# GELU of stages 0 to 2 built from the hyperbolic tangent, with other engines doing the operations around it and the MLP work in later slots

## The reference

```python
def gelu(x):                                     # stage 1; stage 2 uses jax.nn.gelu(x, approximate=True), the same
    return 0.5 * x * (1.0 + jnp.tanh(0.7978845608028654 * x * (1.0 + 0.044715 * x * x)))
...
ln_out = layernorm(x, ln3_s, ln3_b)              # stage 1
mlp_out = gelu(ln_out @ w1 + b1) @ w2 + b2       # 256 -> 1024 -> 256
return x + mlp_out
...
out = rmsnorm(attn_out, postnorm_w)              # stage 2
out = jax.nn.gelu(out @ mlp_w1 + mlp_b1) @ mlp_w2 + mlp_b2
return out + residual
```

## Time and profile before

| what | value |
|---|---|
| median of 3 runs | 2325.23 us (2323.97 to 2326.45) |
| the profiled execution | 2326.19 us |
| its span, first to last instruction | 2324.5 us |
| mean granted clock of PE | 0.961 |
| PE busy | 2114.0 us (91%) |
| DVE busy | 1292.8 us (56%) |
| ACT busy | 1257.4 us (54%) |
| POOL busy | 680.7 us (29%) |

### The profile page before, as it was taken

The page is one execution under the profiler, slowest core; times in us unless marked ns, Lnnn a source line. Parts: engine busy times, 40 slices in busy tenths (PEclk is TensorE's granted clock), DMA queues, the critical chain, the costliest instruction groups (busy, mean ns, idle before and its releaser), DMA issues.

```text
span 2324.5 us, 43553 instructions
## 1 busy us (share of the span) xinstructions
PE 2114.0 (91%) x14880; PEld 1810.9 (78%) x14880; DVE 1292.8 (56%) x4117; ACT 1257.4 (54%) x3924; POOL 680.7 (29%) x618
## 2 busy tenths in 40 slices
PE   4788999999999999897699999999799999999788
PEld 3667777777777777675599999999689999999677
DVE  3658575858576665433455555555545555555654
ACT  2466777786868776644444444444444444444432
POOL 2223333323333333322322222213322221222353
PEclk8899999999999999997799999999999999999989
DMA  6000000000000000000100000000000000000100
GB/s 237 1 4 11 1 10 1 11 1 9 2 2 10 1 4 1 3 1 1 49 24 23 23 18 23 14 23 23 16 24 18 23 14 23 23 23 14 37 14 23
DMA packets 23663, 45.23 MB, mean 19 GB/s; under 512 B 2400, under 2 KB 10080, under 8 KB 22624
## 3 DMA queue, kind: packets, MB, share of 16 engines
q1 hardware_dynamic: 21440, 32.62, 4.5%
q10 hardware_dynamic: 1440, 8.72, 0.9%
q0 software_dynamic: 640, 2.10, 0.3%
HBM read 41.33 MB, written 2.10 MB: 19 GB/s over the span
## 4 chain that ended last, share of the span: by engine, by line
PE 22%; issue 22%; POOL 5%; DVE 2%; ACT 1%; POOLq 0%; ACTq 0%; DVEq 0%
PE general L1573 15%; PE o_psum L1622 2%; PE scores L1610 2%; PE general L1729 2%; POOL probs L1219 1%; POOL w_qk L1195 1%; PE pT_psum L1670 1%; POOL hT L1210 1%; DVE oT L1555 1%; POOL X L1235 1%; POOL w_v L1195 1%; POOL w_o L1195 0%; POOL vrow L1199 0%; DVE oT L1424 0%; ACT oT L1334 0%
## 5 line engine op out<-in xcount | busy, mean ns | idle before, releaser
L430 POOL TENSOR_TENSOR probs<-probs,rsums 128x512 f32<-128x512 f32 (+1 forms) x288 | 283.9, 992 | 670.2 <-DVE rsums L631 669.1
L1219 POOL TENSOR_TENSOR probs<-probs,rsums 128x512 f32<-128x512 f32 x128 | 133.2, 1040 | 764.3 <-DVE rsums L1417 764.3
L470 ACT ACTIVATE probs<-negated,negmax 128x128 f32<-128x128 f32 (+1 forms) x768 | 326.2, 429 | 49.3 <-DVE negmax L622 48.4
L914 PE MATMUL pT_psum<-ident,probs 128*128 128x128 f32 x1088 | 181.8, 290 | 62.1 <-DVE probsT L637 34.4
L1326 ACT COPY probsT<-pT_psum 128x512 f32<-128x512 f32 x128 | 74.9, 585 | 288.8 <-PE pT_psum L1670 288.8
L914 PEld LDWEIGHTS pT_psum<-ident,probs 128*128 128x128 f32 x1088 | 134.0, 148 | 110.6 <-issue 75.2
L1573 PE MATMUL general<-hT,w_qk 128*128 128x512 f32 x768 | 207.0, 405 | 4.2 <-POOL hT L1210 4.2
L1573 PE MATMUL general<-w_o,oT 128*128 128x256 f32 x1536 | 194.6, 281 | 17.0 <-DVE oT L1424 17.0
L1573 PEld LDWEIGHTS general<-w_o,oT 128*128 128x128 f32 x1536 | 186.0, 188 | 25.3 <-DVE oT L1424 18.1
L1573 PE MATMUL general<-ctxT,w_qk 128*128 128x512 f32 x768 | 200.5, 397 | 0.0
L1318 ACT ACTIVATE probs<-scores,negmax 128x128 f32<-128x128 f32 x512 | 180.1, 369 | 29.8 <-DVE negmax L1409 29.7
(11 more groups left out here) (173 smaller groups left out, 4211.2 us busy)
## 6 DMA issues: line engine op xcount, KB each, us to landing
raw_qk<-w_qk_dram SPq DMA_DIRECT2D x34, 256.0 KB, 2.7
raw_v<-w_v_dram SPq DMA_DIRECT2D x17, 256.0 KB, 2.6
raw_vrows<-vrows_dram SPq DMA_DIRECT2D x17, 256.0 KB, 3.2
weights_a<-weights_a_dram ACTq DMA_DIRECT2D x2, 2048.0 KB, 17.7
raw_o<-w_o_dram SPq DMA_DIRECT2D x16, 256.0 KB, 2.6
weights_a<-weights_a_dram ACTq DMA_DIRECT2D x3, 1024.0 KB, 10.0
X<-x_dram SPq DMA_DIRECT2D x8, 256.0 KB, 7.4
ctx_in<-ctx_dram SPq DMA_DIRECT2D x8, 256.0 KB, 4.5
```

Source lines behind the costliest of these rows:

```text
L430: nc.gpsimd.tensor_tensor(pr, pr, rsums[:, n % 4, 0:segs].unsqueeze(2).broadcast_to([P, segs, width(kind) // segs]), ALU.mult).then_inc(s[ ...
L470: last = nc.scalar.activation(probs[:, n % PROBS, i * wide:(i + 1) * wide], src[:, i * wide:(i + 1) * wide], ACT.Exp, scale=1.0 if kind == ...
L914: last = nc.tensor.transpose(pT_psum[:, j * P:(j + 1) * P], probs[:, n % PROBS, j * P:(j + 1) * P], ident[:, :])
L1219: nc.gpsimd.tensor_tensor(pr, pr, rsums[:, t % 2, :].unsqueeze(2).broadcast_to([P, NB, P]), ALU.mult).then_inc(s["probs_ready"], 1)
```

## The change

- The GELU is computed as y (1 + tanh(c y (y y + s))) with y the pre-activation, and the factor 0.5 is applied in the residual sum. ACT writes y to `upT` with `Identity` (`pre_activations`). POOL computes y y, adds s, multiplies by y into the new tile `inner` (`gelu_argument`, in the slot of the up-projection, as the last thing of the slot). ACT applies `Tanh` with a scale to it one slot later (`tanh`), DVE computes (t + 1) y two slots later (`gelu_product`, before the slot's first work).
- The down-projection waits for the product of `up3` (`gelu_ready`).
- `WORK`: the MLP's ups of stage 1 go from slots 24 to 27 to 26 to 29, its downs from 29, 30 to 32, 33; the downs of stage 2 go from 58, 59 to 60, 61; `lat`, `lat_q`, `lat_k` go from 32, 33, 34 to 34, 35, 35; `cross_k` from 8 to 4 and `cross_v` from 13 to 5. The order within slots changes too.
- `ctx_in` and `xhat` have one buffer each; SP loads ctx 1 after all of x, and each later one waits for the group before.

```diff
-        ("mlp2_down0", 58),
-        ("ln3", 23), ("mlp2_down1", 59),
-        ("chan_q", -12), ("chan_k", -12), ("mlp1_up0", 24),
-        ("self_o", 7), ("chan_v", -11), ("mlp1_up1", 25),
-        ("mlp1_up2", 26), ("cross_k", 8),
-        ("ln2", 9), ("mlp1_up3", 27),
-        ("cross_q", 10),
-        ("mlp1_down0", 29),
-        ("mlp1_down1", 30),
-        ("cross_v", 13),
-        ("ln1", -4), ("lat", 32),
-        ("self_q", -3), ("lat_q", 33),
-        ("self_k", -2), ("lat_k", 34),
-        ("self_v", -1), ("lat_o", 53)]
+        ("cross_k", 4),
+        ("ln3", 23), ("cross_v", 5),
+        ("chan_q", -12), ("chan_k", -12), ("mlp2_down0", 60),
+        ("self_o", 7), ("mlp2_down1", 61), ("chan_v", -11),
+        ("mlp1_up0", 26),
+        ("ln2", 9), ("mlp1_up1", 27),
+        ("cross_q", 10), ("mlp1_up2", 28),
+        ("mlp1_up3", 29),
+        ("ln1", -4), ("mlp1_down0", 32),
+        ("self_q", -3), ("mlp1_down1", 33),
+        ("lat", 34), ("self_k", -2),
+        ("lat_q", 35), ("lat_k", 35), ("self_v", -1), ("lat_o", 53)]
+
+GELU_ARGUMENT, GELU_TANH, GELU_PRODUCT = 0, 1, 2
...
-        ctx_in = sb("ctx_in", [P, 2, NA, D])
-
-        xhat_of = {"x": sb("xhat_x", [P, NA, D]), "y": sb("xhat_y", [P, NA, D])}
+        ctx_in = sb("ctx_in", [P, NA, D])
+
+        xhat = sb("xhat", [P, NA, D])
...
+        inner = sb("inner", [P, 2, 2 * RA])
...
+                def gelu_argument(name, g):
+                    i, y, t = up_parts(name, g)
+                    wait_copied(pool, name, g)
+                    wait_count(pool, s["gelu_ready"], i - 1)
+                    nc.gpsimd.tensor_tensor(t, y, y, ALU.mult).then_inc(s["gelu_step"], 1)
+                    pool.wait_ge(s["gelu_step"], 2 * i + 1)
+                    nc.gpsimd.tensor_scalar(t, t, GELU_SHIFT, None, ALU.add).then_inc(s["gelu_step"], 1)
+                    pool.wait_ge(s["gelu_step"], 2 * i + 2)
+                    nc.gpsimd.tensor_tensor(t, t, y, ALU.mult).then_inc(s["argument_ready"], 1)
...
-                        ins = nc.scalar.activation(upT[:, f, :], src[:, j * RA:(j + 1) * RA], ACT.Gelu_apprx_tanh, bias=col(name + "_b", f))
+                        ins = nc.scalar.activation(upT[:, f, :], src[:, j * RA:(j + 1) * RA], ACT.Identity, bias=col(name + "_b", f))
                     ins.then_inc(freed, 1)
+
+                def tanh(name, g):
+                    i, _, t = up_parts(name, g)
+                    act.wait_ge(s["argument_ready"], i + 1)
+                    nc.scalar.activation(t, t, ACT.Tanh, scale=GELU_SCALE).then_inc(s["tanh_done"], 1)
...
+                def gelu_product(name, g):
+                    i, y, t = up_parts(name, g)
+                    dve.wait_ge(s["tanh_done"], i + 1)
+                    nc.vector.scalar_tensor_tensor(out=y, in0=t, scalar=1.0, in1=y, op0=ALU.add, op1=ALU.mult).then_inc(s["gelu_ready"], 1)
...
                         wait_free(pe, name + "_down", g)
-                        for i in (2, 3):
-                            wait_copied(pe, f"{name}_up{i}", g)
+                        pe.wait_ge(s["gelu_ready"], UPS.index((name + "_up3", g)) + 1)
```

More of the change, by code:

```diff
@@ L74 @@
 NEG = -1.0e30
+GELU_CUBIC = 0.044715
+GELU_SHIFT = 1.0 / GELU_CUBIC
+GELU_SCALE = 0.7978845608028654 * GELU_CUBIC
 RSQRT_MAGIC = 1597463007.0
@@ L127, in at_slot, with ups_at @@
             if (slot - after) % PERIOD == 0 and 0 <= (slot - after) // PERIOD < GA]
+def ups_at(slot):
+    return [(name, g) for name, g in at_slot(WORK, slot) if "_up" in name]
 def pair_at(slot):
@@ L145 @@
 ADD_ORDER = [item for slot in SLOTS for item in at_slot(ADDS, slot)]
+UPS = [(name, g) for name, g in WORK_ORDER if "_up" in name]
 MASKED_UNITS = [key for key in UNIT_INDEX if key[0] in ("self", "cross")]
@@ L250, in stages_0_to_2 @@
         ctxT_loaded = [sem(f"ctxT_loaded{i}") for i in range(B // NB)]
-        ctx_loaded = [sem(f"ctx_loaded{i}") for i in range(2)]
         mask_cross_loaded = [sem(f"mask_cross_loaded{i}") for i in range(2)]
@@ L447, in _ @@
                         normalise(kind, g, 2 * p + 1)
+                    for name, g in ups_at(slot - GELU_ARGUMENT):
+                        gelu_argument(name, g)
             @block.scalar
@@ L569, in _ @@
                         copy_out(name, g)
+                    for name, g in ups_at(slot - GELU_TANH):
+                        tanh(name, g)
             @block.vector
@@ L678, in norm @@
                     inverse_root()
-                    xhat = xhat_of[STREAM[name]]
+                    before = NORM_ORDER.index((name, g)) - 1
+                    if before >= 0:
+                        k, n = uses[NORM_ORDER[before]]
+                        dve.wait_ge(full[k], n + 1)
                     for b in range(NA):
@@ L731, in _ @@
                         rsum(kind, g, 2 * p)
+                    for name, g in ups_at(slot - GELU_PRODUCT):
+                        gelu_product(name, g)
                     for name, g in work[:1]:
```

36 lines of the change are left out of this document (22 added, 14 removed).

## The result

| | before | after |
|---|---|---|
| median of the runs | 2324.6 us (4 runs) | 2442.5 us (2439.3 to 2443.6, 4 runs) |
| span of the profiled execution | 2324.5 us | 2440.9 us |
| mean granted clock of PE | 0.961 | 0.938 |

The ratio is 1.0504, 95% interval 1.0486 to 1.0523: the change made the kernel 118 us slower. The forecast was 2379 us with a range to 2430. The sign was right, the size was not.

What follows compares the result with a forecast made beforehand. PE was taken to set the pace. Five periods +32, the end +11, group 6 with slot 149 +12, first groups +6, outside the periods -6, stage 3 -0.7: +54 on 2326.2, median 2379 us, range 2312 to 2430.

Steps and rivals of the forecast that it cites:

- the walk of a period: One steady period of 18 slots (126 us): removed waits -5.25, LayerNorm waits and clock drops added, +6.35 us; five periods +32.
- the three ACT waits: PE waits ending with ACT (0.42, 1.51, 0.89 us), 2.82 a period, forecast to go with the table loads.
- Outside the five periods: Stages 0 to 2 beyond the five steady periods: shorter ACT waits credited with 6 us.
- Class 13: Slots numbered 13 modulo 18, first LayerNorm: PE waits 4.85 us for 1.09, with port +4.5, clock drop +1.7.
- Class 4: Slots numbered 4 modulo 18, third LayerNorm: PE waits 2.65 us for 0.48, with port +3.2, clock drop +1.7.
- the port: SBUF access shared by DVE and POOL: two-input DVE operations wait for POOL's; 0.8 and 1.0 us, 1.8 a period.
- the third rival: Each small operation of a normalisation waits for a POOL operation: some 8 us a period more, +40, 2419 us; chance 0.25.
- Where nothing covers: Places with little other PE work: the end +11, group 6's second MLP with slot 149 +12, slots 27 and 32 +6.
- group 6's second MLP: Slots 163 to 168, nearly alone: four arguments of 13.6 us against some 10 us of PE work, +6.
- Two new drops a period: Lowered PE clock behind the first and third LayerNorm's waits, 1.7 us each.
- The first rival: LayerNorms are not exposed because ACT, DVE and POOL have time free: faster, 2307 us; chance 0.17.
- The signs named: Right: listed ACT, POOL, PE-wait and period values; wrong: period under 124 us, or steady PE waits on POOL's probs or gelu_ready.

Runs made afterwards that it cites:

- old_order: New GELU nearly in the order of the kernel before; only mlp2's downs one slot later and cross_k at 4: 2446.0 us, ratio 1.0521 to before.
- order_alone: Changed order and single buffers, but the kernel before's tanh GELU on ACT with its table loads: 2400.7 us, ratio 1.0336 to before.
- no_addition: Changed kernel without POOL's addition of the constant, its other two operations kept: 2402.0 us, ratio 1.0339 to the kernel before.
- merged_mlp1: Kernel before, own GELU; ACT takes up-projections last in a slot, first MLP's four paired in slots 24, 24, 26, 26: 2305.6 us, ratio 0.9931.
- no_argument_last: Changed kernel without POOL's three GELU operations, DVE's product moved behind the normalisation of its slot: 2363.5 us, ratio 1.0174 to before.
- before_identity: Kernel before with Identity in place of the tanh GELU in stages 0 to 2, so no table loads there: 2274.3 us, ratio 0.979.

## Why the prediction was wrong

The step that failed is the walk of a period, "So a period changes by ... = +6.35, five of them +32 us". Measured were +13.6 a period, 68 for five. The runs give the terms of one way from the kernel before to the changed one, in us a period (four periods of the table, divided by four): loads -6.6, order +6.8, product and tanh +5.1, argument +8.2. The prediction had -5.25 for what goes and +11.6 for all that comes, where 20.1 came. Over the whole span the same way reads -51 + 60 + 31 + 77 = +117. It is one way of several: by old_order the new GELU costs 172 us over Identity, and then the changed order costs nothing more. That the parts exceed the forecast is shown; how much belongs to each depends on what is already there.

**The loads: -29 forecast, -51 measured.** The ACT waits went as read. The step that failed is "the share of the three ACT waits ... and the clock drop behind one of them, 1.7": busy time of PE fell by 4 us a period and not by 1.7, and "Outside the five periods I credit 6 us" was some 20. The reading of the earlier trace rows was inexact: 0.9 us is the idle time ahead of the 50 loads; behind a load the next instruction of ACT starts 0.012 us later (95 of 108 loads of the whole trace).

**The order.** The prediction never priced the order as a whole. Its walk of classes 13 and 4 charged lost cover only where a LayerNorm was seen behind it; by my expectation for order_alone that was 13 us, and 60 (without loads) to 75 (with them) were measured. What the walk left out: the second LayerNorm's full size, the bank of the ctx values, lost cover in fill and drain, where one group has less beside it, and that classes 11 to 13, which lose 9 us of PE work (two halves of a down-projection and cross_v) and get 1.8 back (`mlp1_up3`), are shorter for PE than for the chain of DVE, ACT and POOL, with or without the new operations in it.

**Where it lands.** Class 13: I walked 4.85 us of wait from DVE's side and found 1.40, because another wait of 3.08 at POOL's probabilities stands 6 us ahead of it and delays PE by itself, and the clock that fell behind it slowed PE's work up to the LayerNorm by 1.5 us. I walked one chain, and had named this very wait as a sign that I was wrong. That the sum of both, 4.5 us, is near the 4.85 is luck. Class 4: 2.65 and 1.0 for the port forecast, 4.91 found. Its two products took no 1.5 but 2.9 us, and three of the small operations after them 3.1 us, where an undisturbed one takes 0.16. DVE's timeline:

```profile
500.04 2.94 DVE L748 SCALAR_TENSOR_TENSOR upT<-inner,upT 128x512 f32<-128x512 f32 x2
...
505.04 0.16 DVE L739 TENSOR_TENSOR newton<-newton,var 128x2 f32<-128x2 f32 x1
...
505.63 1.20 DVE L739 TENSOR_TENSOR newton<-newton,var 128x2 f32<-128x2 f32 x1
506.86 0.96 DVE L741 SCALAR_TENSOR_TENSOR rstd<-newton,rstd 128x2 f32<-128x2 f32 x1
507.85 0.96 DVE L737 SCALAR_TENSOR_TENSOR newton<-rstd 128x2 f32<-128x2 f32 x1
508.85 0.16 DVE L739 TENSOR_TENSOR newton<-newton,var 128x2 f32<-128x2 f32 x1
```

This is the port; POOL's timeline shows what ran beside them:

```profile
502.40 1.48 POOL L454 TENSOR_TENSOR inner<-upT 128x512 f32<-128x512 f32 x1
503.97 1.49 POOL L456 TENSOR_SCALAR inner<-inner 128x512 f32<-128x512 f32 x1
505.55 1.26 POOL L458 TENSOR_TENSOR inner<-inner,upT 128x512 f32<-128x512 f32 x1
506.76 2.04 POOL L447 TENSOR_TENSOR probs<-probs,rsums 128x512 f32<-128x512 f32 x2
```

The port costs this one chain 2.6 us (3.12 less three times 0.16), against the 1.0 that I took. The rule of the Trainium skill ("SBUF — State Buffer", Who interferes with whom) that I had put into the third rival holds again beside POOL's products: 1.20 us beside POOL's 1.26. Beside its addition it holds only in part: the operation at 505.04 falls into L456 (503.97 to 505.46) and takes 0.16. In the whole trace 22 of these small operations with two SBUF inputs began in a product of POOL (the normalising of probabilities is one too), and each ended 0.02 us after it. 56 began in an addition: the six within its first 0.17 us ended 0.62 us after its start, the other fifty ran in 0.16.

**POOL's operations.** The addition was bounded by 0.40 and 0.81 us; it takes 1.57. The groups by line of stages 0 to 2:

```profile
L456 POOL TENSOR_SCALAR inner<-inner 128x512 f32<-128x512 f32 x64 | 100.5, 1570 | 5.6
L458 POOL TENSOR_TENSOR inner<-inner,upT 128x512 f32<-128x512 f32 x64 | 83.2, 1301 | 5.4
L454 POOL TENSOR_TENSOR inner<-upT 128x512 f32<-128x512 f32 x64 | 69.6, 1088 | 65.3 <-ACT upT L557 64.8
L748 DVE SCALAR_TENSOR_TENSOR upT<-inner,upT 128x512 f32<-128x512 f32 x64 | 60.3, 949 | 61.1 <-ACT inner L563 61.1
```

One argument is 4.1 us with its gaps and not 3.4, and no_addition shows what that third operation is worth: 40 us. The product, taken as 0.75, takes 0.95 on average: 40 of the 64 took 0.79 to 1.52 us, the other 24 from 0.65 to 0.71, of which two had nothing of POOL beside them (0.69). POOL pays too: its addition takes 1.49 us alone and 1.81 where it begins beside a product of DVE.

**Where nothing covers.** The end was near: +8.5 for the wait and 3 for the clock, 11 in all, against 13.4 measured from slot 174 to the start of stage 3. Its parts were not: POOL's four arguments took 16.7 us and not 13.6, so that PE waits 13.98 us for the last product where 1.02 stood, and the up-projections ahead of it took 8.59 us instead of 10.04:

```profile
1143.86 2.08 PE L950 MATMUL scores<-kT_lat,qm_lat 32*128 32x256 f32 x8 [9.42 <-DVE negmax L658]
...
1222.22 3.33 PE L852 MATMUL general<-weights_a,upT 128*128 128x256 f32 x7 [13.98 <-DVE upT L748]
```

The upper row is group 6's second MLP, for which I had 6 us: DVE's front of the next unit stands behind products that wait for POOL; at the third LayerNorm of slot 149 PE waits 10.08 us, where I had added 6 too. The drain came to 38 us; forecast were these 12 and a part of the fifth period's 6.35. Stage 3 itself became 1.8 us shorter (0.7 forecast).

**The clock.** Two new drops a period were charged, 3.4 us; the time at 1.2 GHz grew by 13.6 us a period, 5 us of PE time. A forecast of where waits arise is also one of clock: in the changed kernel's period each of the five waits of 1.40 us and more had a stretch at 1.2 GHz begin in it or within 1 us behind it. That it need not is shown by merged_mlp1 (below).

**The rivals.** The third (port, 2419) was nearest in time and its place was right, in part: of the argument's 77 us, the port, POOL's queue ahead of the probabilities and the ends each hold a share that was not separated. The first rival, that the LayerNorms are not exposed, is excluded by the trace after (4.91 and 2.54 us at two of them).

**The signs named.** ACT without loads, POOL near 55% (54), 3 us and more in class 5 and the long wait before the last down-projection came true. Not true were ACT at 60 to 70% (55% of the period), 3 us in class 14 (1.40) and a period of 130 to 135 us (139.9); the wait for POOL's probabilities, named as a sign of being wrong, was there.

Open: how the 31 us of product and tanh divide; why PE's busy time changes by more than the clock's record explains.

## What to carry to other kernels

Price a new order by itself, before what it is made for: list for each slot how much work the bounding engine keeps, and compare it with the longest chain of the others in that slot; a slot that is emptied costs where another engine's chain is the longer one. Such a price holds for what stands in the order when it is measured: here it was 75, 60 and 0 us. When several chains end close together, removing one wait can show the next one at nearly full price (no_argument_last), or not (before_identity), so test a part alone (the square of order and function took four kernels and settled what no walk of the trace had). And where only a few of many costly events can be saved, sharing them (two up-projections to one table switch) may win what replacing them loses.

## What had not been expected of the hardware

- POOL's addition of a constant to 128x512 takes 1.49 us undisturbed (1.57 on average), longer than its product of two tensors (1.26 undisturbed, 1.30 on average) and 3.7 times its two-operation form of half the size (0.40 us). Its square, with one tensor read twice, takes 1.04.
- The longest of the three, the addition, holds up DVE the least: operations of DVE with two SBUF inputs that began 0.65 us or more after its start took 0.16 us, as alone, where those that began in one of POOL's products waited for its end (counts in the section above). A whole product of DVE, 0.71 us from 411.31, ran inside an addition of 1.49 us from 410.87.
- A wait of the same length may or may not be followed by the lower clock. In the kernel before, the waits of 1.51 us (oT_x) and 2.41 us (class 17) that recur in every period had a stretch at 1.2 GHz begin in or about 1 us behind them in most periods, but none at 572 and at 594 us. In merged_mlp1, with 0.79 and 1.04 us in place of 1.51 and 0.89, none of the five waits of 2.41 us was followed by one, from 260 to 890 us.
